# Another written-out order of events in a causal attention on TensorE, ScalarE and VectorE

## The chip, the cores and the metric

One NeuronCore of a Trainium2 chip runs the whole kernel in one launch. The metric is the device time in microseconds.

## The reference

The input x has 4 sequences of 2048 rows and 256 columns. A layer norm without weights gives xn. The result is x plus a causal attention of xn (16 heads of 16 columns, rotary positions) plus a feed-forward of xn whose operands are quantised blockwise to 4-bit values.

```python
xn = _layernorm(x, axis=-1)
scores = jnp.einsum('bhqd,bhkd->bhqk', rope(q), rope(k)) * scale
scores = jnp.where(causal, scores, finfo.min)
out = jnp.einsum('bhqk,bhkd->bhqd', softmax(scores), v)
x = x + out @ Wo.T + _L0_ffn_ref(xn, w_gate, w_up, w_down)
```

## The kernel before

Three blocks run one after the other: `norm_ffn_qkv` (norm, feed-forward, the projections with the rotation, and q and k split into three bf16 parts that go to HBM), `attention`, and `out_projection`. Only `attention` and the function that writes down its order are touched.

The attention makes 16 iterations, one for each of the 4 sequences and each group of 4 heads (`HG`). The first 14 are a loop whose body holds two iterations; the last two are written out behind it. In an iteration the 2048 queries are four blocks of 512 (`qb` 0 to 3). Three kinds of work go on:

- **Tiles** find the row maxima ahead of the scores. There are 140 tile events, numbered by block, then by 128 queries (`j`), then by 512 keys (`c`). TensorE multiplies a tile into one of four PSUM banks (`tile`, L1153), and VectorE reduces it: L1322 without a mask (512 columns, one head), L1327 with the causal mask, head by head, on the diagonal (128 columns for four heads in one event, 256 for two heads, 384 or 512 for one). A tile's bank is free for the fourth tile or row after it. After the last tile of a block come `top` (VectorE L1339, then four operations of GpSimd) and `row`: TensorE turns the maxima (L1164) into a tile bank, VectorE copies them (L1344), and SyncE places them by four DMAs as further rows of the queries, so that the scores' matmul subtracts them.
- **Scores**: 160 events, 40 steps of 128 keys times 4 heads. They are called s0a to s39d below: the step and the head a to d. Steps 0 to 3 belong to block 0, 4 to 11 to block 1, 12 to 23 to block 2, 24 to 39 to block 3. TensorE multiplies (L1178) into one of three PSUM banks, 512 columns or, in the four last steps of a block, 512, 384, 256 and 128 with a mask product behind (L1183). ScalarE makes the exponentials (L1247) into a ring of four steps. The score three places later takes the same bank and waits for that exponential.
- **Value products**: one event per step (`weigh`, L1198), four heads in four column groups of TensorE, f32, recorded as two passes for each head, into one bank `acc` for the block. A step waits for its four exponentials, and an exponential waits until the products four steps before are done. After a block's last step ScalarE copies `acc` to SBUF (`take_acc`, L1254), and SyncE stores it (`out`). The next block's first products wait for that copy.

The order of all these is written out: one string `ORDER`, which every engine follows with its own events of the plan. `s` is the next score, `t` the next tile (with the `top` behind it), `r` the next row, `o` the next store. In the kernel before, the products have no letter: they stand in the list of scores, steps n-2 and n-1 ahead of the last head of every even step n, and each takes an `s` of the string. The accumulator's copy has none either: ScalarE makes it where the block's last products stand. A part of the tiles, those before number 74 (`LEAD`), is made in the iteration before the one that uses them; it makes the maxima of blocks 0 and 1 and part of those of block 2, and stands behind tile 139 in the order.

Of the kernel before, what the change touches and what calls it, by code (L numbers as in the profile page):

```python
# [34 lines left out]
HG = 4  # L35
# [12 lines left out]
QB = SEQ // GROUP  # L48
KB = SEQ // P
ITERS = HGS * BATCH  # L50

LEAD = 0.52
ONE_PAIR = float(np.array([0x3F803F80], np.uint32).view(np.float32)[0])
WEIGH_AT, WEIGH_STEPS = 3, 2
ORDER = ("stssttsststtssttsstsssstsststsststsssrtststststststostssstststssttststststsststssttsstststssstss"
         "sttstsststssssttsstttsstststsossssttsstttsststsssstsststttssttssssstststsststtssssstsrtstsststts"
         "tsssstsststsststrssssttssstottstsstsssststtststststststssstststssttsttsstssstssttssrtststsssstss"
         "tststtsttsstssssttsttsstsstsssststssttssttstssstssstttsstsso")


class Chain:
# [61 lines left out]
def norm_ffn_qkv(nc, d, x_all, woT, identf):  # L123


    with ExitStack() as ctx:
# [111 lines left out]

        LEAD = len(lead)
        job_no = {None: numbered(lead), True: numbered(jobs(True)), False: numbered(jobs(False))}  # L240
# [3 lines left out]
        def bank_use(g, more, job):  # L244

            n = job_no[more][job]
            if more is None:
                return n % 2, n // 2
            return (LEAD + n) % 2, g * BANK_JOBS + (LEAD + n) // 2

# [564 lines left out]
def attention_plan():  # L815

    tiles, n = [], 0
    for qb in range(QB):
        for j in range(GT):
            for c in range(qb):
                for h in range(HG):
                    tiles.append(("tile", n, qb, j, c, h, 1, GROUP))
                    n += 1
            heads = (4, 2, 1, 1)[j]  # L830
            for h in range(0, HG, heads):
                tiles.append(("tile", n, qb, j, qb, h, heads, (j + 1) * P))
                n += 1
        tiles.append(("top", qb))

    def cost(e):

        if e[0] != "tile":
            return 0
        return e[6] * e[7] + 64 * (e[6] if e[4] == e[2] else 1)  # L840

    all_cost, first, spent = sum(cost(e) for e in tiles), 0, 0
    while spent < LEAD * all_cost:
        spent += cost(tiles[first])
        first += 1
    events = [(*t, 0) for t in tiles[first:]] + [(*t, 1) for t in tiles[:first]]

    steps = [(qb, kb, kb - 4 * qb if kb >= 4 * qb else None) for qb in range(QB) for kb in range(4 * qb + 4)]

    scores = []  # L850
    for n, (qb, kb, j) in enumerate(steps):
        for h in range(HG):
            if h == WEIGH_AT and n and n % WEIGH_STEPS == 0:
                scores += [("weigh", m, *steps[m]) for m in range(n - WEIGH_STEPS, n)]
            scores.append(("scores", HG * n + h, n, qb, kb, j))
    scores += [("weigh", m, *steps[m]) for m in range(n + 1 - WEIGH_STEPS, n + 1)]


    plan, rows, outs, scored, at = [], [], 0, 0, 0
    for letter in ORDER:  # L860
        if letter == "s":
            plan.append(scores[scored])
            scored += 1
        elif letter == "o":
            plan.append(("out", outs))
            outs += 1
        elif letter == "r":
            plan.append(rows.pop(0))
        else:
            plan.append(events[at])  # L870
            at += 1
            if at < len(events) and events[at][0] == "top":
                rows.append(("row", *events[at][1:]))
                plan.append(events[at])
                at += 1
    assert scored == len(scores) and at == len(events) and outs == QB and not rows

    for qb in range(QB):
        start = next(n for n, e in enumerate(plan) if e[0] == "scores" and e[3] == qb)
        assert all((n < start) == (not e[2]) for n, e in enumerate(plan) if e[0] == "row" and e[1] == qb)  # L880
    return plan, len(steps)
# [69 lines left out]
def attention(nc, d, identf, qs0, ks0, ahead, sums, pickb, recips):  # L951

    plan, STEPS = attention_plan()
    HEAD_STEPS = HG * STEPS
    SCORE_SLOTS, TILE_SLOTS, PROB_STEPS = 3, 4, 2 * WEIGH_STEPS
    PROB_SLOTS = PROB_STEPS * HG
    ROW_COLS, ROW_LANDS = HG * PARTS * GT, HG * 16
    ahead_places = {e: n for n, e in enumerate(e for e in plan if e[0] in ("tile", "row") and e[-1])}
# [3 lines left out]
    last_step = {e[2]: e[1] for e in plan if e[0] == "weigh"}  # L962
# [10 lines left out]
    with ExitStack() as ctx:  # L973
# [3 lines left out]
        def sem(name):  # L977
            return ctx.enter_context(nc.semaphore(name))
# [3 lines left out]
        tile = ctx.enter_context(nc.psum_tensor("tile", [P, TILE_SLOTS, GROUP], F32))  # L982
# [25 lines left out]
        pv_done = sem("pv_done")  # L1008
# [222 lines left out]
        def _(act):  # L1231
# [15 lines left out]
                nc.scalar.activation(prob[:, k % PROB_SLOTS, 0:width], score[:, k % SCORE_SLOTS, 0:width],  # L1247
                                     ACT.Exp, scale=HEAD ** -0.5).then_inc(probs_ready, 1)

            def take_acc(it, e):  # L1250
                act.wait_ge(pv_done, it * STEPS + e[1] + 1 + PROB_STEPS)
                qb = e[2]
                act.wait_ge(out_stored[qb % 2], it * (QB // 2 * 16) + qb // 2 * 16 + 1)
                nc.scalar.copy(acc_sb[:, qb % 2, :], acc[:]).then_inc(acc_taken, 1)  # L1254

            def iteration(it):
                for e in plan:
                    if e[0] == "scores":
                        exponentials(it, e)
                    elif e[0] == "weigh" and e[1] == last_step[e[2]]:  # L1260
                        take_acc(it, e)

            for it in range(ITERS):
                iteration(it)
# [297 lines left out]
```

## Time and profile before

| | |
|---|---|
| median of 3 runs | 2565.34 us (2563.74, 2568.26, 2565.34) |
| span of the profiled execution | 2561.9 us |
| its own time | not listed apart from the runs; the lowest of them is 1.8 us over the span |
| first block, to the attention's first tile | 829 us |
| attention, from its first score (874.8) to its last product | 1597.8 us |
| an inner iteration | 99.73 to 99.89 us |

The span goes from the first traced instruction to the last. A page gives each engine's busy time in it. Timelines and windows count us from the span's start. Here, a row of a timeline is a run of like instructions, with its start, its length to the end of the last one, and the count; the numbers of a line (L1153) are those of the kernel's listing above. PEld is TensorE's weight loader, which runs beside its matmuls.

### The profile page before, as it was taken

What the parts mean: (1) busy time and instruction counts of PE and PEld (TensorE: products, weight loads), DVE (VectorE), ACT (ScalarE), POOL (GpSimd) and SP (SyncE); (2) the same over time, 40 slices, a digit from 0 to 9 for tenths busy, and PEclk for the clock granted to TensorE, in tenths of its full rate; (3) what the DMA queues carried; (4) which work ended last, traced back from release to release, by engine and by line L of the source; (5) the groups of instructions that cost most, each with busy time, mean ns of one, the idle gap of its engine ahead of it and who ended that gap; (6) DMA issues with size and microseconds to landing.
All of it is one profiled execution on the core that took longest, in us unless ns stands there. A gap on an engine that the chain in (4) does not pass through costs nothing. (4 is left out here: it accounts for less than half of the span.)

```text
span 2561.9 us, 51480 instructions
## 1 busy us (share of the span) xinstructions
PE 2440.4 (95%) x14338; PEld 1170.2 (46%) x14338; DVE 2236.7 (87%) x4841; ACT 1594.3 (62%) x3260; POOL 166.3 (6%) x466
## 2 busy tenths in 40 slices
PE   5999999999996999999999999999999999999987
PEld 3555555555564234434444344344344344443335
DVE  8999999999996989898899899889888888998834
ACT  3545554554552277777777777777777777777740
POOL 2001101101101000000000000000000000000010
PEclk8999999999998699999999999999999999999999
DMA  6212112122123412212112122122122121120034
GB/s 199 74 56 67 64 64 69 56 70 71 54 72 90 113 35 61 70 33 67 43 54 73 31 62 67 35 62 74 35 61 69 33 68 41 55 61 6 20 125 173
DMA packets 141411, 168.57 MB, mean 66 GB/s; under 512 B 14048, under 2 KB 107536, under 8 KB 141200
## 3 DMA queue, kind: packets, MB, share of 16 engines
q1 hardware_dynamic: 137856, 159.49, 19.9%
q10 hardware_dynamic: 3344, 6.41, 0.7%
q8 instruction: 115, 1.88, 0.3%
q14 instruction: 96, 0.79, 0.1%
HBM read 97.17 MB, written 67.90 MB: 64 GB/s over the span
## 5 line engine op out<-in xcount | busy, mean ns | idle before, releaser
L1247 ACT ACTIVATE prob<-score 128x512 f32<-128x512 f32 (+3 forms) x2560 | 1158.6, 542 | 390.2 <-PE score L1178 192.1
L1322 DVE TENSOR_REDUCE top<-tile 128x1 f32<-128x512 f32 x1536 | 956.8, 680 | 104.0 <-PE tile L1153 95.7
L1178 PE MATMUL score<-qs,ks 99*128 99x512 bf16 (+3 forms) x2560 | 812.6, 350 | 7.8 <-ACT prob L1247 3.1
L1153 PE MATMUL tile<-ks,qs 96*128 96x512 bf16 (+3 forms) x2560 | 778.0, 355 | 25.7 <-DMA ks<-qkp 16.5
L1198 PE MATMUL acc<-prob,vs 128*32 128x512 f32 (+3 forms) x5120 | 535.3, 536 | 0.0
L1327 DVE CUSTOM_DVE_ANT_0 tile<-tile,mask 128x128 f32<-128x128 f32 (+3 forms) x1024 | 469.5, 518 | 61.5 <-PE tile L1153 59.3
L1178 PEld LDWEIGHTS score<-qs,ks 99*128 99x128 bf16 x2560 | 244.6, 97 | 414.5 <-ACT prob L1247 225.6
L1153 PEld LDWEIGHTS tile<-ks,qs 96*128 96x128 bf16 x2560 | 239.0, 98 | 298.0 <-DVE top L1322 84.6
L349 PE MATMUL gu<-wguT,xT 128*128 128x512 f32 (+1 forms) x768 | 310.7, 557 | 0.0
L1198 PEld LDWEIGHTS acc<-prob,vs 128*32 128x32 f32 x5120 | 133.9, 109 | 244.1 <-issue 138.9
L1183 PE MATMUL score<-identb,maskb 128*128 128x128 bf16 x1024 | 212.2, 220 | 0.0
L349 PEld LDWEIGHTS gu<-wguT,xT 128*128 128x128 f32 x768 | 143.6, 190 | 144.9 <-issue 122.8
L393 PE MATMUL misc<-wdT,hT 128*128 128x256 f32 x768 | 178.9, 383 | 1.3 <-ACT hT L472 1.3
L393 PEld LDWEIGHTS misc<-wdT,hT 128*128 128x128 f32 x768 | 143.8, 190 | 31.4 <-issue 11.3
L1327 DVE DVE_READ_ACCUMULATOR2_ANT top<- 128x1 f32 x1024 | 140.2, 137 | 0.0
L375 PE MATMUL misc<-xT,wqkvT_sb 128*128 128x512 f32 x256 | 118.4, 606 | 7.5 <-ACT xT L472 7.5
L1183 PEld LDWEIGHTS score<-identb,maskb 128*128 128x128 bf16 x1024 | 100.8, 98 | 38.7 <-issue 0.7
L1285 POOL CAST top_parts<-topm 128x16 bf16<-128x16 f32 x64 | 16.3, 254 | 1495.6 <-DVE topm L1339 1495.6
L492 ACT ACTIVATE silu<-gu 128x704 f32<-128x704 f32 x64 | 48.2, 753 | 90.0 <-PE gu L349 90.0
L109 DVE SCALAR_TENSOR_TENSOR scaled<-magic,scaled 128x704 f32<-128x704 f32 (+1 forms) x96 | 78.6, 818 | 19.2 <-ACT magic L477 19.2
L472 ACT COPY hT<-misc 128x512 f32<-128x512 f32 (+1 forms) x128 | 58.0, 482 | 58.1 <-PE misc L389 57.4
L477 ACT ACTIVATE magic<-scaled 128x704 f32<-128x704 f32 (+1 forms) x96 | 70.9, 738 | 30.4 <-DVE scaled L100 30.3
(130 smaller groups left out, 1723.0 us busy)
## 6 DMA issues: line engine op xcount, KB each, us to landing
qkp<-parts SPq DMA_DIRECT2D x192, 128.0 KB
vscr<-vt SPq DMA_DIRECT2D x16, 1024.0 KB, 5.4
vs<-vscr SPq DMA_DIRECT2D x16, 1024.0 KB, 6.1
oscr<-acc_sb SPq DMA_DIRECT2D x64, 256.0 KB, 2.1
qs<-qkp SPq DMA_DIRECT2D x64, 192.0 KB, 3.4
ks<-qkp SPq DMA_DIRECT2D x64, 192.0 KB, 3.3
x_all<-in_x SPq DMA_DIRECT2D x16, 512.0 KB, 9.0
qs<-qkp SPq DMA_DIRECT2D x64, 128.0 KB, 3.1
```

The source lines that it names most:

```text
L109: link(nc.vector.scalar_tensor_tensor(out=scaled, in0=magic, scalar=1.25 * MAGIC, in1=scaled, op0=ALU.max, op1=ALU.add))
L349: mm = nc.tensor.matmul(gu[:, t % 2, c0:c0 + w], xT[:, KT + k, t * P:(t + 1) * P], wguT[:, k, c0:c0 + w], start=(k == 0), stop=(k == KT - 1))
L375: mm = nc.tensor.matmul(bank, wqkvT[:, k, t * P:(t + 1) * P], xT[:, k, :], start=(k == 0), stop=(k == KT - 1))
L393: mm = nc.tensor.matmul(bank[:, 0:DIM], hT[:, t % 2, i, :], wdT[:, i, :], start=(i == 0), stop=(i == IT - 1))
L477: nc.scalar.activation(magic[:, par, 0:w], scaled[:, par, 0:w], ACT.Abs, scale=MAGIC).then_inc(magic_ready, 1)
L1153: mm = nc.tensor.matmul(bank[:, h * width:(h + 1) * width], qs[par][0:ROWS, h0 + h, q0:q0 + P], ks[par][0:ROWS, h0 + h, k0:k0 + width], st ...
L1178: mm = nc.tensor.matmul(bank[:, 0:width], ks[par][0:ROWS_M, h, kb * P:(kb + 1) * P], qs[par][0:ROWS_M, h, qb * GROUP + off:(qb + 1) * GROU ...
L1183: mm = nc.tensor.matmul(bank[:, 0:P], maskb[:], identb[:], start=False, stop=True, skip_group_check=True)
L1198: mm = nc.tensor.matmul(acc[h * VW:(h + 1) * VW, off:GROUP], vs[par][:, kb // GT, kb % GT, h, :], prob[:, (HG * n + h) % PROB_SLOTS, 0:GRO ...
L1247: nc.scalar.activation(prob[:, k % PROB_SLOTS, 0:width], score[:, k % SCORE_SLOTS, 0:width], ACT.Exp, scale=HEAD ** -0.5).then_inc(probs_r ...
L1322: nc.vector.tensor_reduce(top[:, j, h0, c:c + 1], bank, AX.X, ALU.max).then_inc(tile_taken, 1)
L1327: last = nc.vector.tensor_tensor_reduce(out=head, in0=head, in1=mask[:, GROUP - width:GROUP], scale=1.0, scalar=MASK, op0=ALU.add, op1=ALU ...
```

## The change

`ORDER` is another string, with two letters more. `w` is the products of the next step; they are no longer bound to a place between scores. `a` is the copy of the accumulator (`take`) together with its store. The products stand as 2, 2, 3, 3, 2, 1, 2, 2, 3, 2, 2, 3, 1, 2, 2, 2, 2 and 4 steps at a time. The first tile of the iteration is named by its number, 74. The ring of four steps of exponentials keeps its size.

```diff
--- before.py
+++ after.py
@@ -49,13 +49,12 @@
 KB = SEQ // P
 ITERS = HGS * BATCH
 
-LEAD = 0.52
+AHEAD = 74
 ONE_PAIR = float(np.array([0x3F803F80], np.uint32).view(np.float32)[0])
-WEIGH_AT, WEIGH_STEPS = 3, 2
-ORDER = ("stssttsststtssttsstsssstsststsststsssrtststststststostssstststssttststststsststssttsstststssstss"
-         "sttstsststssssttsstttsstststsossssttsstttsststsssstsststttssttssssstststsststtssssstsrtstsststts"
-         "tsssstsststsststrssssttssstottstsstsssststtststststststssstststssttsttsstssstssttssrtststsssstss"
-         "tststtsttsstssssttsttsstsstsssststssttssttstssstssstttsstsso")
+ORDER = ("sttssttsttsststswwtsssttsststsstssswwrtaststssttststststswwwststssttssttssttststsstswwwtsststsst"
+         "stssstttsstswwstsstasttststwtssttsststtswwstsstststttstswwststssttstststswwwrtststssttststsststs"
+         "tsswwsststsststtssswwstsstsatsttststwwwststtssttststswststsststttstswwtsststststtststwwtstssrrst"
+         "tstsststtstwwstsststtstststststsstwwtssttstsststsststsswwwwa")
 
 
 class Chain:
@@ -833,36 +832,23 @@
                 n += 1
         tiles.append(("top", qb))
 
-    def cost(e):
-
-        if e[0] != "tile":
-            return 0
-        return e[6] * e[7] + 64 * (e[6] if e[4] == e[2] else 1)
-
-    all_cost, first, spent = sum(cost(e) for e in tiles), 0, 0
-    while spent < LEAD * all_cost:
-        spent += cost(tiles[first])
-        first += 1
+    first = tiles.index(next(e for e in tiles if e[0] == "tile" and e[1] == AHEAD))
     events = [(*t, 0) for t in tiles[first:]] + [(*t, 1) for t in tiles[:first]]
 
     steps = [(qb, kb, kb - 4 * qb if kb >= 4 * qb else None) for qb in range(QB) for kb in range(4 * qb + 4)]
-
-    scores = []
-    for n, (qb, kb, j) in enumerate(steps):
-        for h in range(HG):
-            if h == WEIGH_AT and n and n % WEIGH_STEPS == 0:
-                scores += [("weigh", m, *steps[m]) for m in range(n - WEIGH_STEPS, n)]
-            scores.append(("scores", HG * n + h, n, qb, kb, j))
-    scores += [("weigh", m, *steps[m]) for m in range(n + 1 - WEIGH_STEPS, n + 1)]
-
-
-    plan, rows, outs, scored, at = [], [], 0, 0, 0
+    scores = [("scores", HG * n + h, n, *step) for n, step in enumerate(steps) for h in range(HG)]
+    weighs = [("weigh", n, *step) for n, step in enumerate(steps)]
+
+    plan, rows, outs, scored, weighed, at = [], [], 0, 0, 0, 0
     for letter in ORDER:
         if letter == "s":
             plan.append(scores[scored])
             scored += 1
-        elif letter == "o":
-            plan.append(("out", outs))
+        elif letter == "w":
+            plan.append(weighs[weighed])
+            weighed += 1
+        elif letter == "a":
+            plan += [("take", outs), ("out", outs)]
             outs += 1
         elif letter == "r":
             plan.append(rows.pop(0))
@@ -873,7 +859,7 @@
                 rows.append(("row", *events[at][1:]))
                 plan.append(events[at])
                 at += 1
-    assert scored == len(scores) and at == len(events) and outs == QB and not rows
+    assert scored == len(scores) and weighed == len(steps) and at == len(events) and outs == QB and not rows
 
     for qb in range(QB):
         start = next(n for n, e in enumerate(plan) if e[0] == "scores" and e[3] == qb)
@@ -952,7 +938,7 @@
 
     plan, STEPS = attention_plan()
     HEAD_STEPS = HG * STEPS
-    SCORE_SLOTS, TILE_SLOTS, PROB_STEPS = 3, 4, 2 * WEIGH_STEPS
+    SCORE_SLOTS, TILE_SLOTS, PROB_STEPS = 3, 4, 4
     PROB_SLOTS = PROB_STEPS * HG
     ROW_COLS, ROW_LANDS = HG * PARTS * GT, HG * 16
     ahead_places = {e: n for n, e in enumerate(e for e in plan if e[0] in ("tile", "row") and e[-1])}
@@ -1247,9 +1233,8 @@
                 nc.scalar.activation(prob[:, k % PROB_SLOTS, 0:width], score[:, k % SCORE_SLOTS, 0:width],
                                      ACT.Exp, scale=HEAD ** -0.5).then_inc(probs_ready, 1)
 
-            def take_acc(it, e):
-                act.wait_ge(pv_done, it * STEPS + e[1] + 1 + PROB_STEPS)
-                qb = e[2]
+            def take_acc(it, qb):
+                act.wait_ge(pv_done, it * STEPS + last_step[qb] + 1 + PROB_STEPS)
                 act.wait_ge(out_stored[qb % 2], it * (QB // 2 * 16) + qb // 2 * 16 + 1)
                 nc.scalar.copy(acc_sb[:, qb % 2, :], acc[:]).then_inc(acc_taken, 1)
 
@@ -1257,8 +1242,8 @@
                 for e in plan:
                     if e[0] == "scores":
                         exponentials(it, e)
-                    elif e[0] == "weigh" and e[1] == last_step[e[2]]:
-                        take_acc(it, e)
+                    elif e[0] == "take":
+                        take_acc(it, e[1])
 
             for it in range(ITERS):
                 iteration(it)
```

## Rows read from the trace of the kernel before

**Rows 1.** Page, busy time and share of the span of each engine.
```profile
PE 2440.4 (95%) x14338; PEld 1170.2 (46%) x14338; DVE 2236.7 (87%) x4841; ACT 1594.3 (62%) x3260; POOL 166.3 (6%) x466
```

**Rows 2.** Windows, four inner iterations: length, busy (count) by engine, granted clock, DMA share.
```profile
1175.93:1275.82 99.89, 99.39 (x712) 40.83 (x709) 89.71 (x234) 74.69 (x165) 4.02 (x16) 1.00 0.19 55
1275.82:1375.55 99.73, 99.43 (x708) 41.12 (x709) 89.08 (x232) 74.35 (x164) 4.03 (x16) 1.00 0.18 55
1375.55:1475.29 99.74, 99.37 (x712) 40.66 (x709) 89.67 (x234) 74.66 (x165) 4.03 (x16) 1.00 0.19 55
1475.29:1575.00 99.71, 99.43 (x708) 41.13 (x708) 89.11 (x233) 74.39 (x164) 4.04 (x16) 1.00 0.18 55
```

**Rows 3.** Timeline of TensorE, a group of 512 and 512 columns: start, length, count.
```profile
1139.31 1.92 PE L1198 MATMUL acc<-prob,vs 128*32 128x512 f32 x16
1141.17 0.39 PE L1178 MATMUL score<-qs,ks 99*128 99x512 bf16 x1
```

**Rows 4.** Timeline of TensorE, a group of 256 and 128 columns and its neighbours.
```profile
1304.08 0.38 PE L1178 MATMUL score<-qs,ks 99*128 99x512 bf16 x1
1304.30 0.38 PE L1153 MATMUL tile<-ks,qs 96*128 96x512 bf16 x1
1304.52 0.38 PE L1178 MATMUL score<-qs,ks 99*128 99x512 bf16 x1
1304.83 0.86 PE L1198 MATMUL acc<-prob,vs 128*32 128x256 f32 x16
1305.62 0.39 PE L1178 MATMUL score<-qs,ks 99*128 99x512 bf16 x1
1305.85 0.38 PE L1153 MATMUL tile<-ks,qs 96*128 96x512 bf16 x1
```

**Rows 5.** Timelines of VectorE and TensorE at the start of an iteration (at 1076.21).
```profile
1077.45 1.89 DVE L1322 TENSOR_REDUCE top<-tile 128x1 f32<-128x512 f32 x3 [0.68 <-PE tile L1153]
1079.26 0.69 DVE L1327 CUSTOM_DVE_ANT_0 tile<-tile,mask 128x512 f32<-128x512 f32 x1
...
1076.21 0.39 PE L1178 MATMUL score<-qs,ks 99*128 99x512 bf16 x1 [0.29 <-issue]
...
1076.49 0.38 PE L1153 MATMUL tile<-ks,qs 96*128 96x512 bf16 x1
1076.71 0.38 PE L1178 MATMUL score<-qs,ks 99*128 99x512 bf16 x1
...
1076.99 0.38 PE L1178 MATMUL score<-qs,ks 99*128 99x512 bf16 x1
...
1079.07 0.33 PE L1178 MATMUL score<-qs,ks 99*128 99x384 bf16 x1
...
1079.30 0.33 PE L1178 MATMUL score<-qs,ks 99*128 99x384 bf16 x1
...
1079.52 0.38 PE L1153 MATMUL tile<-ks,qs 96*128 96x512 bf16 x1
1080.06 0.39 PE L1153 MATMUL tile<-ks,qs 96*128 96x512 bf16 x1 [0.16 <-DVE top L1327]
```

**Rows 6.** Timeline around step 25, third head; in brackets idle before and its releaser.
```profile
1235.39 0.59 ACT L1254 COPY acc_sb<-acc 128x512 f32<-128x512 f32 x1
...
1235.87 1.60 ACT L1247 ACTIVATE prob<-score 128x512 f32<-128x512 f32 x3
1235.91 1.00 PE L1178 MATMUL score<-qs,ks 99*128 99x512 bf16 x3
...
1236.52 0.10 PEld L1178 LDWEIGHTS score<-qs,ks 99*128 99x128 bf16 x1 [0.51 <-ACT prob L1247]
```

**Rows 7.** Timeline around tiles 39 and 40.
```profile
1247.78 0.73 DVE L1327 CUSTOM_DVE_ANT_0 tile<-tile,mask 128x512 f32<-128x512 f32 x1
...
1248.17 0.60 PE L1153 MATMUL tile<-ks,qs 96*128 96x512 bf16 x2
...
1248.43 0.73 DVE L1327 CUSTOM_DVE_ANT_0 tile<-tile,mask 128x512 f32<-128x512 f32 x1
...
1248.82 0.84 PE L1153 MATMUL tile<-ks,qs 96*128 96x512 bf16 x2
```

**Rows 8.** Timeline of weight loads in the group of rows 4.
```profile
1304.30 0.10 PEld L1178 LDWEIGHTS score<-qs,ks 99*128 99x128 bf16 x1
1304.83 0.59 PEld L1198 LDWEIGHTS acc<-prob,vs 128*32 128x32 f32 x16 [0.43 <-ACT prob L1247]
```

**Rows 9.** Timelines of VectorE: first tile after a group, unmasked and masked reductions in runs.
```profile
1158.41 3.73 DVE L1322 TENSOR_REDUCE top<-tile 128x1 f32<-128x512 f32 x6 [0.94 <-PE tile L1153]
...
1207.60 0.60 DVE L1327 CUSTOM_DVE_ANT_0 tile<-tile,mask 128x384 f32<-128x384 f32 x1
...
1208.11 0.60 DVE L1327 CUSTOM_DVE_ANT_0 tile<-tile,mask 128x384 f32<-128x384 f32 x1
...
1302.13 0.39 PE L1153 MATMUL tile<-ks,qs 96*128 96x512 bf16 x1
...
1302.56 3.70 DVE L1322 TENSOR_REDUCE top<-tile 128x1 f32<-128x512 f32 x6 [0.33 <-PE tile L1153]
```

**Rows 10.** Timeline of ScalarE in the last iteration.
```profile
2450.65 4.03 ACT L1247 ACTIVATE prob<-score 128x512 f32<-128x512 f32 x8 [1.19 <-PE score L1178]
2455.86 0.60 ACT L1247 ACTIVATE prob<-score 128x512 f32<-128x512 f32 x1 [1.19 <-PE score L1178]
```

## The prediction

> **What bounds the kernel now.** The page's busy shares [rows 1] say TensorE (95%), with VectorE close (87%). The change touches only the attention, so I cut its 16 iterations out by windows [rows 2]. An inner one takes 99.73 to 99.89 us, with TensorE busy 99.4, VectorE 89.1 to 89.7 and ScalarE 74.5 at a granted clock of 1.00 (the 2.4 GHz level). A TensorE that is 99.5% busy still need not be at its peak, because the ends of its matmuls are modelled. So I count its columns and take the remainder. Per iteration the scores stream 69,632 columns, the tiles 69,632, the masks 8,192 and the rows 512. The value products hold 17,408 columns, four heads side by side.
>
> Their price: a group of two steps of 512 columns lasts 1.86 us from its start to the next matmul's [rows 3], one of 256 and 128 columns 0.79 us [rows 4]. The difference, 1.07 us for 640 columns, is four columns' time at 2.4 GHz per column (1.067), so value products cost 17,408 x 4 = 69,632. The sum is 217,600 columns, 90.7 us. The 388 other matmuls follow each other at 0.22 us where 512 columns take 0.213 [rows 4]; at 0.0055 us each (rounding allows 0.004 to 0.007) that is 2.1 us.
>
> A group has a price of its own: 0.79 less 0.64 for its 384 x 4 columns is 0.15 us, and its first matmul comes 0.31 us after the score before it instead of 0.22, another 0.09. That is 0.24 us per group, 4.8 us for 20 groups. 90.7 + 2.1 + 4.8 = 97.6; the 2.1 us left of 99.73 are waits of TensorE.
>
> Three kinds of these waits, which the timeline shows:
> - The loops' back edges, every second iteration. VectorE's first reduction starts 1.24 us after the iteration's first score, although its tile had been issued at 0.28 [rows 5]. So tile 81, which needs the bank of tile 77, waits 0.3 us beyond its turn: its predecessor is issued at 1079.52, it at 1080.06, where 0.22 is normal. TensorE itself stands 0.29 us before its first score, put down to issue: its own edge. Together 0.61 us in every second iteration, 0.3 us in each.
> - The accumulator copy. ScalarE copies at 1235.39 and can exponentiate s24d only at 1235.87; the weight load of s25c, which needs that bank, comes at 1236.52 after 0.51 us idle of the loader [rows 6]. Three scores' matmuls that would take 0.82 us (two spacings of 0.22 and a last one of 0.38) take 1.00: 0.18 us.
> - The ring of four tile banks. In the run of tiles 39 and 40 two matmuls take 0.84 us where two take 0.60 [rows 7]: 0.24 us.
>
> These are 0.7 us; the rest are some twenty waits, most under 0.1.
>
> **The change part by part.**
>
> *Groups.* Before: 20 groups of two steps. The new string has 18: two of one, eleven of two, four of three, and the four last steps (36 to 39) together. No column, matmul, exponential, reduction or DMA is added or removed, and the split between iterations is the same (tile 74 is also where 0.52 of the cost falls), so prologue and work per iteration are as before. Two groups fewer: 2 x 0.24 = 0.48 us per iteration. From below: if entering and leaving cost only the 0.09 that is seen at the entry, twice, it is 0.36. From above 0.48, since the rest of a group is columns.
>
> *A rule that speaks against this.* The 16 loads of the short group lie within its 0.79 us beside its matmuls, 0.59 us busy [rows 8], and of its length only 0.15 us is not columns. By the Trainium skill, "TensorE: Matmul & The Clock Gate", section "Part 3: Packing small matmuls", a weight load overlaps running matmuls only when its row group differs. Here all loads use all 128 rows, so by this rule each pass would show its load, the cost would be per step, and merging would save nothing. The trace disagrees: beside columns the group has 0.15 us, and a load for each of its four passes would be 4 x 0.10 us at the duration of a load [rows 8].
>
> *The order: waits of TensorE.* I laid durations end to end along the new order. Reductions follow each other at 0.61 us (3.73 less 0.68, over five [rows 9]), masked 512-column ones at 0.65 [rows 7]; exponentials at 0.49 (4.03 less 0.60, over seven [rows 10]). A bank comes free 0.80 us after a masked reduction's start [rows 5], a score bank 0.65 after an exponential's [rows 6]; VectorE starts 0.43 us after the first tile following a group [rows 9]. This way of laying gives the old tile 81 too: tile 77's reduction starts at 3.05, plus 0.80 is 3.85, and the row has 3.85.
>
> New start: s0a, t74, t75, s0b, s0c, t76, t77, s0d, t78, t79, s1a, s1b, t80, s1c, t81. Scores of 512 with mask take 0.28, of 384 0.22, tiles 0.22, so t81's turn is at 3.32. VectorE starts t74 at 0.71 if its back edge is hidden, t77 at 2.54, bank free at 3.34: a wait of 0.02. Its edge is hidden: after the group 34-35 come the rest of four backlogged tiles (2.3 less the group's 1.9, 0.4), three masked ones of 0.51 [rows 9] and five of 0.61, 5.0 us in all. TensorE needs 3.4 us for the stretch's scores, masks and tiles and 2.4 for the last group (1,280 columns x 4, and 0.24); VectorE is done 0.8 us before the end and its edge took 0.68. TensorE's edge is hidden likewise: its branch follows the issue of step 39, whose wait is for s39d, and steps 36 to 38 (1.9 us) now lie between them. The third copy moves behind s26a, when step 23 has long been done: the 0.18 goes. The others move little.
>
> Four more stretches laid so: group 4-6 to 10 (0.1 us of waits), 15 to 22 (0.06), 24-26 to 32 (0.05 and 0.2, before tiles 46 and 50). About 51 of 97 us walked, 0.44 us of waits; for the whole I take 0.8. Gain 2.1 - 0.8 = 1.3. Bounds: none left, 2.1; nothing gained, 0 or a little below.
>
> *What the longer groups cost the others.* In three steps (2.8 us) VectorE empties four banks (2.4) and then stands about 1 us, until the first tile and 0.43 more. By my stretches that happens at groups 4-6, 7-9, 24-26 and the last; elsewhere its backlog covers the group. VectorE has 97.1 - 89.4 = 7.7 us of idle to give. ScalarE stands too, with over 20 us to give. Value products wait for the exponentials of their last step; where a group now follows directly on them (s1d, s6d, s19d, s39d) the earlier steps of the group cover it except before step 1, at most 0.2 us.
>
> *SyncE.* Output stores are issued with the copies, which only wait for later points; both rows of the next iteration come at 80 us instead of 56 and 78 by the same sums, 17 us before the first score that reads them. Nothing.
>
> *The last iteration.* From tile 139 on it has no tiles and ScalarE sets the pace: eight exponentials, then 1.19 us idle, period 5.21 us [rows 10]. Three steps would take 7.84 (12 x 0.48 + 0.04 + 2.04), against 7.81 at today's pace. No gain there; I give this iteration 0.
>
> **Sum.** 15 x (0.48 + 1.3) = 26.7 us. Profiled span 2561.9 - 26.7 = 2535.2. The median of the runs is 3.4 us over the span, which lies around the traced instructions and is unchanged: 2538.6, said as 2538. The 0.8 is the soft term: 0.3 more or less of it is 4.5 us.
>
> **The rivals.**
> - *Only the groups.* The new order has new waits of 2.1 us in places I did not walk; 15 x 0.48 = 7.2 gained: 2558. For: every order with VectorE at 92% has waits. Against: the walked half.
> - *The price is per step*, not per group (the rule above): only 15 x 1.3 = 19.5 gained, 2546. Against: the columns account for all but 0.15 us.
> - *The gain is eaten.* Waits of 2.6 us per iteration, 0.5 over today's, at tile banks in the long runs between groups (before the products of step 20: ten tiles, a row and a block maximum, 6.7 us of VectorE in 4.7 us): 2565, no change.
> - *VectorE starves behind long groups*, slower. Today it idles 10.3 us per iteration, 0.5 per group. If each group keeps 0.5 and the four of three and the last add 0.85 each, it idles 9 + 4.3 = 13.3, an iteration is 89.4 + 13.3 = 102.7, 15 x 3.0 = 45 us more: 2610. It decides once VectorE idles over 10.3 us per iteration. For: it idles behind groups of two already (0.33 us [rows 9]). Against: by the sums most new stretches leave it a backlog that outlasts the group.
>
> **How the numbers follow.** Forecast 0.58, only groups 0.14, per step 0.08, eaten 0.12, starving 0.08. A measurement of this kernel tells 0.2% (5.1 us) from no change. Faster: 0.58 + 0.14 + 0.08 = 0.80; same 0.12; slower 0.08. The low end is no wait left at all: 15 x 2.58 = 39, 2526. The high end takes in the groups alone, 2558; what lies above has 0.2.
>
> **What would show it.** Inner iterations of 97.9 us in the windows. The first matmul behind a group of three full steps 2.71 us after the group's start (2.56 for the columns, 0.15) if the price is per group, 2.79 if per step. No idle "issue" before s0a; tile 81 on its turn; VectorE's busy time unchanged, its idle down to about 8.5 us. The forecast is wrong if an inner iteration takes over 99 us: then the idle before TensorE's loads and who ended it tell "groups only" and "eaten" (tile banks) from "starving" (VectorE idle over 10.3 us, waiting for tiles).

## The result and the profile after

The changed kernel takes 2555.02 us (four runs, 2554.96 to 2555.31) against 2565.8 us before, run beside it (four runs, 2563.74 to 2568.26): a ratio of 0.9951, interval 0.9937 to 0.9965. Run again later, beside other runs of before, it gave 0.9954 (0.9940 to 0.9968). It is faster, by 11 to 13 us (0.5%) and not by the 27 of the forecast; the interval leaves out 1 both times.

The page and the windows of four inner iterations, as in [rows 1] and [rows 2]:

```profile
PE 2436.1 (95%) x14338; PEld 1173.7 (46%) x14338; DVE 2238.4 (88%) x4841; ACT 1580.6 (62%) x3260; POOL 166.4 (7%) x466
```

```profile
1175.80:1274.54 98.74, 98.72 (x713) 41.03 (x709) 89.58 (x232) 73.61 (x164) 4.04 (x16) 1.00 0.19 55
1274.54:1373.11 98.57, 98.55 (x713) 41.05 (x709) 89.35 (x232) 73.56 (x164) 4.04 (x16) 1.00 0.19 56
1373.11:1472.09 98.98, 98.81 (x713) 40.98 (x709) 89.68 (x232) 73.57 (x164) 4.04 (x16) 1.00 0.19 55
1472.09:1570.64 98.55, 98.53 (x713) 41.02 (x709) 89.35 (x232) 73.57 (x164) 4.04 (x16) 1.00 0.19 55
```

The busy share of TensorE stands at 95% as before and tells nothing. The first column does. Over twelve inner iterations the mean is 98.67 us where it was 99.75; 97.9 had been forecast. VectorE's busy time stayed at 89.5. So the missing 0.8 us are in every iteration, not in one place at the end.

Where the span's 8.4 us (2561.9 to 2553.5) came from: the attention, here from the first score to the start of the last product, went from 1597.5 to 1581.9 us (-15.6). The stretch ahead of it, whose code is the same, was 3.7 us longer, and the tail from there to the end 3.5 us longer (89.6 to 93.1). The first of these is no effect of the change: in the profiles of kernels that don't differ there the first score comes anywhere from 874.2 to 880.0 us. The second is partly one, as shown below. In the second profile of the changed kernel (e_after) the attention took 1581.0 us, the tail 93.7, and the first score came at 876.9. Two single falls of the granted clock to the 1.2 GHz level, 3.4 us each, lie in these numbers as well: one in iteration 14 of before, one in the last iteration of after (windows over these iterations have a granted clock of 0.98 where their neighbours have 1.00); e_after has neither.

For the waits I took every distance between matmuls of the twelve iterations and subtracted the columns at 2.4 GHz, the issue price and the group price of the prediction. What is left, in mean us per iteration:

| | before | after | forecast |
|---|---|---|---|
| waits of TensorE | 2.15 | 1.55 | 0.8 |
| of those listed (over 0.025 each): before scores | 0.93 | 1.02 | |
| before tiles | 0.98 | 0.34 | |

The largest of after: s5c 0.18, s33d 0.11, tile 64 0.09, s25a 0.08, s33a 0.08, tile 2 0.08, s21d 0.08, tile 63 0.07, s7d 0.06, and sixteen of 0.03 to 0.05. Before, the largest were tile 5 0.20, tile 40 0.22, s25c 0.18, tile 81 0.17, s0a 0.16, s36b 0.14; all six are gone. The change cleared the tile banks and put as many waits before scores as there had been.

The group of three full steps, on TensorE:

```profile
1288.08 0.39 PE L1164 MATMUL score<-qs,ks 99*128 99x512 bf16 x1
1288.40 2.78 PE L1184 MATMUL acc<-prob,vs 128*32 128x512 f32 x24
1291.11 0.39 PE L1164 MATMUL score<-qs,ks 99*128 99x512 bf16 x1
```

From 1288.40 to 1291.11 are 2.71 us, and 0.32 stand ahead of it. The start of an iteration, as in [rows 5]:

```profile
1273.99 0.62 PE L1184 MATMUL acc<-prob,vs 128*32 128x256 f32 x12
1274.54 0.39 PE L1164 MATMUL score<-qs,ks 99*128 99x512 bf16 x1
...
1275.24 1.89 DVE L1307 TENSOR_REDUCE top<-tile 128x1 f32<-128x512 f32 x3 [1.35 <-PE tile L1139]
...
1277.40 0.38 PE L1139 MATMUL tile<-ks,qs 96*128 96x512 bf16 x1
...
1277.85 0.39 PE L1139 MATMUL tile<-ks,qs 96*128 96x512 bf16 x1
```

s0a has no idle "issue" any more, VectorE starts 0.70 us after it instead of 1.24, and tile 81 is issued at 1277.85, 3.31 us in (3.32 had been laid for it; 3.85 before).

Now three places where after waits. First s5c; in brackets is the idle time before and what ended it:

```profile
1284.36 0.38 PE L1164 MATMUL score<-qs,ks 99*128 99x512 bf16 x1
...
1284.47 0.60 ACT L1239 COPY acc_sb<-acc 128x512 f32<-128x512 f32 x1
...
1284.93 1.62 ACT L1233 ACTIVATE prob<-score 128x512 f32<-128x512 f32 x3
...
1285.23 0.79 PE L1164 MATMUL score<-qs,ks 99*128 99x512 bf16 x2
1285.62 0.10 PEld L1164 LDWEIGHTS score<-qs,ks 99*128 99x128 bf16 x1 [0.51 <-ACT prob L1233]
```

Two scores take 0.79 us where two take 0.60. The second is s5c, whose bank s4d had. The copy of block 0 stands in ScalarE's queue ahead of s4d's exponential, which so starts at 1284.93, 0.57 us after its matmul at 1284.36. Second s7d, behind the group above, and third s25a:

```profile
1291.60 2.06 ACT L1233 ACTIVATE prob<-score 128x512 f32<-128x512 f32 x4 [2.11 <-PE score L1164]
...
1291.99 0.65 PE L1164 MATMUL score<-qs,ks 99*128 99x512 bf16 x2
1292.25 0.10 PEld L1164 LDWEIGHTS score<-qs,ks 99*128 99x128 bf16 x1 [0.37 <-ACT prob L1233]
```

```profile
1332.18 0.91 PE L1164 MATMUL score<-qs,ks 99*128 99x512 bf16 x3
...
1332.70 0.10 PEld L1164 LDWEIGHTS score<-qs,ks 99*128 99x128 bf16 x1 [0.39 <-ACT prob L1233]
```

0.65 for two instead of 0.60, 0.91 for three instead of 0.82: small sums, each ended by an exponential.

### The profile page after: what moved, and what is told of

The parts are those of the page before. It is cut to its first block and busy times, and to the rows that moved or that the text cites. A ratio compares the mean times of both kernels' runs of the same rounds, so it can differ in the third digit from the quotient of the medians.

```text
span 2553.5 us, 51480 instructions
## 1 busy us (share of the span) xinstructions
PE 2436.1 (95%) x14338; PEld 1173.7 (46%) x14338; DVE 2238.4 (88%) x4841; ACT 1580.6 (62%) x3260; POOL 166.4 (7%) x466
## 5 line engine op out<-in xcount | busy, mean ns | idle before, releaser
L1184 PE MATMUL acc<-prob,vs 128*32 128x512 f32 (+3 forms) x5120 | 528.8, 535 | 0.1
L1312 DVE CUSTOM_DVE_ANT_0 tile<-tile,mask 128x128 f32<-128x128 f32 (+3 forms) x1024 | 473.3, 523 | 46.0 <-PE tile L1139 41.7
L1312 DVE DVE_READ_ACCUMULATOR2_ANT top<- 128x1 f32 x1024 | 147.8, 144 | 0.0
L1169 PEld LDWEIGHTS score<-identb,maskb 128*128 128x128 bf16 x1024 | 100.6, 98 | 34.6 <-issue 0.5
```

The costliest lines, as they stand in the source:

```text
L1169: mm = nc.tensor.matmul(bank[:, 0:P], maskb[:], identb[:], start=False, stop=True, skip_group_check=True)
L1184: mm = nc.tensor.matmul(acc[h * VW:(h + 1) * VW, off:GROUP], vs[par][:, kb // GT, kb % GT, h, :], prob[:, (HG * n + h) % PROB_SLOTS, 0:GRO ...
L1312: last = nc.vector.tensor_tensor_reduce(out=head, in0=head, in1=mask[:, GROUP - width:GROUP], scale=1.0, scalar=MASK, op0=ALU.add, op1=ALU ...
```

## The experiments

Two theories stood against each other. A: the missing 0.75 us per iteration are ScalarE's, because exponentials queue up behind each other, and behind the copy, in places where I had set each score only against its own exponential. B: they are VectorE's, through the four tile banks. Beside them stood the price of a group and of the edges between iterations. "The old order" is the order of before written in the new letters, each store right behind its copy. Order strings are cut to the place that differs.

### Two steps of products moved in the old order (e_tail)

```diff
-...ststssttssttstswwtssstttsstwwa
+...ststssttssttststssstttsstwwwwa
```

Steps 36 and 37 join 38 and 39 at the end.

> The order of before for all scores, tiles, rows and copies (each copy's store directly behind it), with one edit: the products of steps 36 and 37 stand with those of 38 and 39 at the end, one group of four. The prediction's own steps say: one group fewer (0.24 us) and both back edges hidden (0.3 us), so an inner iteration of 99.73 - 0.54 = 99.2 us and about 2557 us in all. The rival: VectorE and ScalarE have no more work laid up for 2.4 us, so what the edges and the group give comes back as waits for tile banks and score banks behind it; inner iteration 99.6 to 100.1 us, total within 5 us of before.

Measured 2568.68 us against 2563.72, ratio 1.0018 (1.0009 to 1.0028). Inner iterations take 99.91 us, before 99.75. The edge's waits (s0a 0.16, tile 81 0.17) are gone and one group less saves 0.23, and all that is lost again: new waits before tile 69 0.18, tile 71 0.18, tile 72 0.30 and tile 73 0.08. TensorE and VectorE there:

```profile
1271.89 1.30 PE L1139 MATMUL tile<-ks,qs 96*128 96x512 bf16 x3
...
1273.35 0.39 PE L1139 MATMUL tile<-ks,qs 96*128 96x512 bf16 x1
1273.67 2.36 PE L1184 MATMUL acc<-prob,vs 128*32 128x512 f32 x32
```

```profile
1272.62 3.07 DVE L1307 TENSOR_REDUCE top<-tile 128x1 f32<-128x512 f32 x5
1276.67 1.46 DVE L1307 TENSOR_REDUCE top<-tile 128x1 f32<-128x512 f32 x2 [0.98 <-PE tile L1139]
```

Three tiles take 1.30 us where three take 0.82: without a group in their midst VectorE cannot catch up, and behind the four steps it stands 0.98 us. The long last group hides the edges, but pays only with the tiles ahead of it spread anew, as the change has them.

### Long groups parted (e_split)

```diff
-...swwwststss...   ...swwwtsstst...   ...swwwrtstst...   ...twwwststts...   ...ststsswwwwa
+...swwswtstss...   ...swwtwsstst...   ...swwrtwstst...   ...twwswtstts...   ...ststswwswwa
```

> The order of after with each group of three parted by one tile or score (two steps, one event, one step) and the last group of four parted by s39d: 23 groups instead of 18, everything else in its place. If a group has a fixed price of 0.24 us: inner iteration 98.7 + 5 x 0.24 = 99.9 us, total 2555 + 15.5 x 1.2 = 2573 us; less where a wait is absorbed. If the price is per step, or merging only moves waits: 98.7 us and 2555 us, and the matmul behind a group of two 0.075 us per step beyond its columns.

Measured 2573.85 us against 2563.72, ratio 1.0038 (1.0024 to 1.0053), inner iterations of 100.31 us. That is 1.64 over after with five groups more. 0.49 of it are waits (a row behind step 18, 0.29; s0a 0.25 back; the rest small, both ways), so a group costs (1.64 - 0.49)/5 = 0.23 us. A single full step parted from its two:

```profile
1192.49 1.92 PE L1184 MATMUL acc<-prob,vs 128*32 128x512 f32 x16
...
1194.35 0.39 PE L1164 MATMUL score<-qs,ks 99*128 99x512 bf16 x1
...
1194.67 1.06 PE L1184 MATMUL acc<-prob,vs 128*32 128x512 f32 x8
...
1195.66 0.39 PE L1139 MATMUL tile<-ks,qs 96*128 96x512 bf16 x1
```

1.86 and 0.99 us against 2.71 for the three together: 0.14 for the second exit, and 0.32 ahead of each group where 0.22 is normal. The change's own saving per group is settled.

### Half the columns for ScalarE, for VectorE, and for both (e_act, e_dve, e_both)

e_act makes its exponentials over the first half of the columns (the rest of the ring holds ones). e_dve reduces half of each tile's columns, and scales the exponent by 1e-30 so that no value overflows. e_both does both. All else is as in after.

```diff
-nc.scalar.activation(prob[..., 0:width], score[..., 0:width], ...
+nc.scalar.activation(prob[..., 0:width // 2], score[..., 0:width // 2], ...
```
```diff
-nc.vector.tensor_reduce(top[:, j, h0, c:c + 1], bank, AX.X, ALU.max)
+nc.vector.tensor_reduce(top[:, j, h0, c:c + 1], bank[:, 0:GROUP // 2], AX.X, ALU.max)
```

> After, with each exponential made over the first half of its columns only (the other half of the ring is filled once with ones), so ScalarE's work is about 40% shorter and its output is not the attention's. Theory A, that the waits I did not foresee are mostly those of scores for ScalarE (three score banks): an inner iteration falls by over half of the 1.57 us of waits, to 97.9 us or less, and idle ended by the exponentials goes. Theory V, that they are mostly tile banks waiting for VectorE: it stays at 98.3 us or more.

> After, with each tile reduced over the first half of its columns only (the row maxima are then not those of all keys, and the exponentials' scale is set near zero so that they stay finite), so VectorE's work is about 40% shorter. Theory A: the inner iteration falls by less than 0.5 us (98.2 us or more), since the scores' waits stay. Theory V: to 97.6 us or less.

> After, with exponentials and tile reductions over half of their columns both (outputs not the attention's). TensorE's waits for either should all go: what is left is columns 90.7 us, 388 matmuls x 0.0055 and 18 groups x 0.23 to 0.24 us, 97.0 us for an inner iteration. If the sum missed a cost of TensorE's own, it stays above 97.3.

One run of each: 2533.19, 2528.05 and 2504.45 us. The last two are not to be set against after as wholes, since their first score comes at 858.3 and 861.3 us. An inner iteration of each, in this order, with the mean over twelve 97.75, 98.43 and 96.95:

```profile
1169.88:1267.64 97.76, 97.72 (x712) 41.23 (x708) 89.41 (x232) 53.34 (x164) 4.01 (x16) 1.00 0.18 56
```

```profile
1154.43:1252.84 98.41, 98.39 (x713) 41.10 (x709) 59.70 (x232) 73.60 (x164) 4.04 (x16) 1.00 0.18 56
```

```profile
1152.67:1249.60 96.93, 96.93 (x712) 41.53 (x709) 59.70 (x232) 53.51 (x164) 4.06 (x16) 1.00 0.19 56
```

Relieving ScalarE gives 0.92 us per iteration, relieving VectorE 0.24, both 1.72; so 0.56 comes only when both are relieved. In e_act the remaining 0.63 of waits are all before tiles, in e_dve the remaining 1.31 nearly all before scores. A has the larger part. VectorE's part is not small, though: with ScalarE out of the way tile 50 waits 0.12 (0.03 in after) and tile 38 0.08 (0.03), so each covers some of the other. These runs say whose the waits of after are; which of them the prediction should have had is told by the third order below. With both relieved nothing waits, and the iteration is what columns, issue and 18 groups make: 97.12 by the prediction's prices, 96.95 measured. That 0.17 is the error of the base sum; counted from 96.95 the waits of after are 1.72 and those of before 2.32, and their difference is the same.

### The copy of block 2 earlier, in the old order (e_copy)

```diff
-...trswwasttssstttstsstsww...
+...trswwsttssstttstasstsww...
```

> The order of before with one edit in it: block 2's copy of the accumulator stands ahead of s26a instead of directly behind the products of steps 22 and 23 (each copy's store directly behind it). The prediction's step: the wait of 0.18 us before s25c goes and nothing takes its place, inner iteration 99.75 - 0.18 = 99.57 us. The rival: ScalarE has to make the copy (0.48 us) somewhere among exponentials of 0.49 us each, and the next block's first products wait for it; the wait reappears before a later score or before the products of step 24, inner iteration 99.7 us or more.

2567.10 us (one run), inner iterations of 99.90. The copy now stands ahead of s26a, near where the change has it. The three scores at step 25 flow, and the tiles behind them don't:

```profile
1236.18 0.39 PE L1164 MATMUL score<-qs,ks 99*128 99x512 bf16 x1
1236.40 0.60 PE L1139 MATMUL tile<-ks,qs 96*128 96x512 bf16 x2
1236.84 0.81 PE L1164 MATMUL score<-qs,ks 99*128 99x512 bf16 x3
1237.49 0.82 PE L1139 MATMUL tile<-ks,qs 96*128 96x256 bf16 x5
```

Three scores in 0.81 us instead of 1.00 [rows 6]: the wait of s25c is gone. In its place tile 23 waits 0.11, tile 24 0.05 more, and step 24's products 0.13. A wait of 0.18 that is removed in front of a VectorE at 90% comes back within ten events. In the change s25c does not wait; there the whole stretch was laid anew, and s25a waits 0.08.

### Shorter copies (e_short)

All copies of the accumulator take 64 of the 512 columns; the outputs of the rest are left at ones.

```diff
-nc.scalar.copy(acc_sb[:, qb % 2, :], acc[:])
+nc.scalar.copy(acc_sb[:, qb % 2, 0:64], acc[:, 0:64])
```

> After, with each accumulator copy made over 64 of its 512 columns only (the rest of the stored block is filled once with ones, so the output is not the attention's). If the wait of 0.18 us before s5c, which the prediction did not have, is block 0's copy in ScalarE's queue ahead of s4d, it goes to under 0.05, and the inner iteration to 98.67 - 0.18 = 98.5 us. If it is the plain rate of the exponentials, it stays at 0.15 or more.

2548.62 us (one run), inner iterations of 98.51, that is 0.16 less. The wait of s5c (0.18) is gone; tile 96 has a new one of 0.07. So the copy's place in ScalarE's queue was the cause at s5c, and of the others it was none: s33d, s25a, s33a and s21d are unchanged.

### The last store first (e_store)

In the last iteration SyncE issues the last block's store ahead of the loads of the reciprocals instead of behind.

```diff
                        if more is False and e[1] == last:
                            keep_recips()
                        store(it, e)
+                        if more is False and e[1] == last:
+                            load_kept_recips()
```

> After, with one edit in SyncE's queue of the last iteration: the last output store is issued ahead of the three loads of reciprocals, not behind them. In after, SyncE issues that store at 2463.46, 2.1 us behind the copy's end, since it comes from the block 2 store, 24 loads, three stores, their landing and six loads, in order. If that queue sets the end of the attention, the store comes 1.5 to 2.7 us earlier and the total falls by up to 2 us (2553). The rival: the output projection's loads start at the same time anyway, or wait for the reciprocals' loads, which are now later: no change, 2555.

2550.13 us (2548.86 to 2550.41) against 2564.78, ratio 0.9943 (0.9925 to 0.9961). That cannot be told from the changed kernel's 0.9951 and 0.9954, and its first score came 4.3 us earlier than after's (874.2 and 878.5 us). So the traces have to decide. What the tail does in before, in after and in e_store, on SyncE's queue:

```profile
2435.19 0.34 SPq L1061 DMA_DIRECT2D oscr<-acc_sb  x1
...
2470.88 2.69 SPq L935 DMA_DIRECT2D recips<-rscr  x6
2473.68 0.36 SPq L1061 DMA_DIRECT2D oscr<-acc_sb  x1
2476.25 2.84 SPq L909 DMA_DIRECT2D last_sums<-oscr  x4
```

```profile
2424.97 0.34 SPq L1047 DMA_DIRECT2D oscr<-acc_sb  x1
2425.36 13.74 SPq L915 DMA_DIRECT2D qs<-oscr  x16
2439.15 10.24 SPq L915 DMA_DIRECT2D ks<-oscr  x8
2449.58 3.41 SPq L1069 DMA_DIRECT2D rscr<-sum_parts  x3
2460.66 2.69 SPq L921 DMA_DIRECT2D recips<-rscr  x6
2463.46 0.36 SPq L1047 DMA_DIRECT2D oscr<-acc_sb  x1
2465.93 2.83 SPq L895 DMA_DIRECT2D last_sums<-oscr  x4
```

```profile
2456.92 0.34 SPq L1047 DMA_DIRECT2D oscr<-acc_sb  x1
2457.38 2.72 SPq L921 DMA_DIRECT2D recips<-rscr  x6
2462.40 2.83 SPq L895 DMA_DIRECT2D last_sums<-oscr  x4
```

From block 2's store to the issue of the last one SyncE needs 38.5 us in both kernels (2435.19 to 2473.68, 2424.97 to 2463.46), for 24 loads, 3 stores, their landing and 6 loads; another 2.5 us later come the projection's first loads. So these loads are bound to block 2's store, and not to the last product:

| | block 2's store ahead of the last product's end | first loads behind it | sum |
|---|---|---|---|
| before | 37.4 | 3.7 | 41.1 |
| e_copy | 34.6 | 6.3 | 40.9 |
| after | 35.7 | 5.2 | 41.0 |
| e_after | 34.0 | 6.9 | 41.0 |
| e_act | 28.3 | 12.7 | 41.0 |
| e_tail | 37.3 | 4.4 | 41.7 |

In the six other kernels in which this queue keeps its order the sum is 40.7 to 41.1. e_copy and e_tail both have each store right behind its copy; e_copy alone has the later copy of block 2, so it is this copy's place, which the change has too, that costs. In after the fall of the clock lies between that store and the last product: it made the last iteration 1.7 us longer and the way to the loads 1.7 us shorter. From the first of these loads to the end pass 85.5 to 87.7 us in all profiles, 85.7 in before and 87.6 in after; that is the other half of the 3.5 us of the tail, and no effect of the change that a run shows.

The last store of after comes 2.1 us after its copy ends (2461.34). With the store moved ahead it goes out 0.1 us after the copy, and the loads still come 6.2 us after the last product (2456.2). The trace shows what they wait for then: the reciprocals' loads, issued until 2460.1, of which the last lands at 2461.93; the loads start at 2462.40. The rival of the expectation came true. Only the order within the queue changed, not its length (41.9 us from block 2's store to these loads).

### A third order (e_best, e_best2)

The string was found by laying each engine's queue end to end with its measured durations and its backlog, and by changing it letter by letter. This sum gives 99.88, 98.52, 100.08, 100.22 for before, after, e_tail and e_split (measured 99.75, 98.67, 99.91, 100.31). Those four were known when it was made; 97.5 for this order was not. The groups are 2, 2, 2, 3, 3, 2, 1, 2, 3, 2, 2, 1, 1, 2, 3, 2, 2, 1 and 4: 19, one more than after.

```diff
-sttssttsttsststswwtsssttsststsstssswwrtaststss...
+tstssttstststsswwsststsststsstssswwststststtsatsststwwsrstts...
```

> After with a third order, laid out so that each engine's queue is carried along the whole iteration, ScalarE's backlog and the copies with it: 19 groups (2,2,2,3,3,2,1,2,3,2,2,1,1,2,3,2,2,1,4), one more than after. Laying the measured durations along it gives an inner iteration of 97.5 us (98.5 for after, where the trace has 98.67; 99.9 for before, 99.75). If the remaining difference is waits for queues that can be foreseen in this way: 97.6 us, and 2555 - 16 = 2539 us. If what I foresee is only as good as in the prediction (0.56 got of 1.3): 98.2 us, 2548 us. If group count alone decides: 98.9 us, slower than after.

> The third order again, beside after: 16 us less than after in either theory, since its inner iteration was 97.61 against 98.67 (15 x 1.06); ratio to before 0.988.

2534.27 us (2531.14 to 2534.66) against 2564.78, ratio 0.9883 (0.9865 to 0.9900); again, on the chip of e_after, 2537.31, ratio 0.9882 (0.9867 to 0.9897), 18.8 us under the changed kernel there. Inner iterations of 97.61 us with 0.26 of waits (s15d 0.10, tile 2 0.07, tile 32 0.07):

```profile
1169.75:1267.48 97.73, 97.73 (x709) 40.88 (x708) 89.54 (x232) 73.94 (x165) 4.04 (x16) 1.00 0.18 56
```

It beats both kernels, with a group more than after: of the 1.06 us per iteration that it has over after, the waits give 1.29 and the extra group takes 0.23. Its last iteration takes 94.1 us, before 96.1.

### The changed kernel again (e_after), and SyncE's queue in the third order (e_best_sp)

e_after is after, unedited. e_best_sp is e_best with the reciprocals' stores between the 16 and the 8 loads, their loads behind both, and so nothing ahead of the last store:

```diff
-                        if more is False and e[1] == last:
-                            keep_recips()
...
+                                if g == QB:
+                                    keep_recips()
+                            load_kept_recips()
```

> The changed kernel itself once more, on one chip with the runs beside it. Its attention took 15.6 us less than before's in the two profiles (1597.5 and 1581.9 us), yet its whole span only 8.4 less: the stage ahead of the attention, which the change does not touch, ended at 878.5 us instead of 874.8, and the tail behind it took 93.1 instead of 89.6. In eight experiments that stage ended at 874.2 to 876.2. If the 878.5 was that run's own, the ratio to before comes out at 0.994 to 0.995 (12 to 15 us); if the new order itself costs at the front, at 0.996 (10 to 11 us) with a start at 878 again. The inner iteration is 98.67 in either case.

> The third order, with SyncE's queue of the last iteration in another order: the stores of the reciprocals' parts stand between the 16 loads into q's buffer and the 8 into k's, and their loads behind the 8, so that the last output store has nothing ahead of it. If SyncE's queue is what holds the end of the attention (6.3 us from the last product to ScalarE's first load of the projection, against 3.9 in before), that stretch falls to 4 us and the total by about 2 us against e_best2. If the stretch is bound by the landing of the last store alone, no change.

e_after: 2556.08 us (2553.34 to 2556.58) against 2568.70, ratio 0.9954 (0.9940 to 0.9968), inner iterations of 98.67 again. e_best_sp: 2538.16 us, ratio 0.9882 (0.9867 to 0.9897), nothing gained on e_best2.

```profile
2436.63 4.64 SPq L921 DMA_DIRECT2D recips<-rscr  x6
...
2445.63 0.59 ACT L1243 COPY acc_sb<-acc 128x512 f32<-128x512 f32 x1 [2.04 <-PE acc L1188]
2446.31 0.36 SPq L1047 DMA_DIRECT2D oscr<-acc_sb  x1
2451.14 2.80 SPq L895 DMA_DIRECT2D last_sums<-oscr  x4
```

The store leaves at once, with nothing ahead of it in SyncE's queue, and now 4.8 us pass to the loads behind it, where they were 2.5 in after: it lands 4.5 us after its issue (2450.81) where it took 2.2. The reciprocals' loads, issued 5 us earlier than in e_best2, are not ruled out: the last two landed only at 2449.32 and 2450.57, some 10 us after their issue, where all six took 2.2 to 2.4 us in after. What held both back stays open. The loads start 5.6 us after the last product, in e_best2 6.0.

## Why the prediction was wrong, point by point

- *What bounds the kernel.* Right. Columns, issue and groups make 97.12 us for the new order; with both other engines relieved 96.95 were measured. The waits of before, read as 2.1, were 2.15.
- *Groups, 0.24 us each, 0.48 per iteration.* Right: 0.23 each by e_split, and the group of three takes the 2.71 us that were named, not 2.79. By the rule of the Trainium skill that the prediction set against this ("TensorE: Matmul & The Clock Gate", section "Part 3: Packing small matmuls"), a load with the same row group doesn't overlap, so merging steps would save nothing; the trace and e_split (0.23 us per group, 2.71 for three steps) disagree with it for these products.
- *The edges, the copy of block 2, tile 40: 0.7 us of named waits gone.* Right, all of them, and tile 5, tile 12 and s36b went with them, which had not been named.
- *"About 51 of 97 us walked, 0.44 us of waits; for the whole I take 0.8."* This is the step that failed: the waits left in the new order, put at 0.8 us per iteration, measured 1.55. About 0.7 are in the stretches that I had walked (the last of them taken up to tile 50), and 0.8 in the other half, for which I had taken 0.36. So the waits fell by 0.60 us (2.15 to 1.55) where 1.3 had been laid, 15 x 0.7 = 10.5 us too little. e_act shows whose they mostly are. The walk asked for each score whether its bank's own exponential, started 0.42 us after its matmul, was done (of this the prediction shows only the rate of the exponentials, 0.49, and no place where one waits behind another). It did not carry what stands ahead of it in ScalarE's queue: behind the copy of block 0 s4d's exponential starts 0.57 us after its matmul (e_short: wait gone without the copy; s5c itself lies in the half that I did not walk), in runs of scores closer together than 0.49 us each one slips further, and behind the group of three the first starts 0.49 and not 0.42 us after its score (1291.11 to 1291.60). In the walked stretches about 0.47 of the waits are before scores. Those before tiles were the smaller part (0.34 in the whole iteration), but not where I had them: of the 0.25 us before tiles 46 and 50 came 0.03, at tile 50. That the backlog was what was missing is borne out by the third order: laid with it, 97.5 us were expected and 97.61 measured. How much of the other half's 0.8 is the same backlog, and how much a price set too low without walking, stays open.
- *Where the rest of the miss lies.* From span to span the forecast was 18.3 us too low (2535.2, measured 2553.5): 9.4 us in iterations 0 to 14, 1.7 the fall of the clock in the last, 3.5 the tail, and 3.7 ahead of the attention, which is no part of the change. The last three the prediction did not have.
- *SyncE: "Nothing."* Wrong, by 1.5 us in one profile and 3.3 in the other. I had looked at the rows of the queries and not at the last iteration, where block 2's store opens a queue of 38.5 us that ends with the last store, and the later copy of block 2 starts it later.
- *The last iteration: no gain.* Right: 96.1 before, 96.2 in e_after. It was 97.8 in the first profile, where the granted clock fell to the 1.2 GHz level for 3.4 us. Iterations 0 and 14 gave 1.7 and 2.2 us there, but in iteration 14 before has the same fall of the clock (103.2 us; 101.8 in e_copy, which has none), and in e_after iteration 0 gave 0.9.
- *The median 3.4 us over the span.* Wrong by 1.6: what lies around a span is 1.8 us in each run, and the rest was that the profiled execution was the fastest of the three. This error made the forecast longer, and so hid as much of the miss.
- The rivals: "only the groups" (waits stay at 2.1, 2558 us) came nearest in time, but not in mechanism, since the waits of before did go and others came. "Starving" did not happen: VectorE idles 98.67 - 89.5 = 9.2 us per iteration, under 10.3.

The sum by measured terms: 15 x 1.1 = 16 us in the attention, less the 3.5 and 4.1 of the tail in the two profiles (SyncE's 1.5 and 3.3 among them), gives 12 to 13. Measured 11 and 13. That the first profile's span is only 8.4 us shorter comes from the 3.7 us ahead of the attention.

## What to carry to other kernels

When an order is laid by hand, carry the backlog of every queue that an event passes, ScalarE's as well as VectorE's, with copies in it; testing each event against its own producer finds the big waits and misses the many small ones, here 1.02 us per iteration before scores, where 1.08 were gained. The part of an order that was not walked should be priced at least like the walked part, and rather worse. Waits at an engine that is 90% busy move when one place is mended (e_tail, e_copy): judge an order as a whole, and look at what the last pass of the loop releases on the DMA queue: a copy moved 2.8 us nearer to the end (e_copy) moved the loads behind the loop by 2.6.

## What the hardware showed that I had not expected

- Exponentials of 512 columns in a run start 0.48 us apart, while the time on record of one grows along the run, so that ends are 0.49 us apart: the run of three in after takes 1.62, of four 2.06.
- A copy by ScalarE of 0.60 us lets the next exponential start 0.46 us after it.
- From the issue of one small store to the loads that wait for it passed 2.5 us when it followed six others in SyncE's queue, and 4.8 us when it followed none (it landed after 2.2 and 4.5 us); two small loads issued 5 to 7 us ahead of the latter took 10 us to land. The cause is open.
- Between the first score of an iteration and its last product, no wait at all is left on TensorE when the two other engines work on half the columns (e_both), though VectorE still is busy for 62% of the time (59.7 of 96.9 us).
